# Row-wise self-attention on one core: all y adds on GpSimd, one PSUM bank per group, one output pair and the copy of g moved

## The reference

```python
xn = (x - moving_mean) * jax.lax.rsqrt(moving_var + BN_EPS) * gamma + beta
q = xn @ Wq + bq
k = xn @ Wk + bk
v = xn @ Wv + bv
scores = jnp.einsum('bhid,bhjd->bhij', q, k) * d ** (-0.5)
attn = jax.nn.softmax(scores, axis=-1)
out = jnp.einsum('bhij,bhjd->bhid', attn, v)
out = out @ Wo + bo
return xn + out
```

## Time and profile before

| | |
|---|---|
| median of 3 runs | 4906.45 us (4906.04 to 4907.05) |
| profiled execution | 4908.15 us, its span 4906.1 us |
| busy: PE, DVE, ACT, POOL | 4865.9, 4404.1, 4353.9, 4509.1 us |
| granted TensorE clock, mean | 0.999 of full speed |
| busy share of the 16 DMA engines, q1 | 82.1% |

### The profile page before, as it was taken

How to read it: one execution, slowest core, us unless ns; L and a number is a source line. 1 busy time by engine, 2 the same in 40 slices (tenths; PEclk the granted TensorE clock), 3 DMA queues, 4 the chain that set the end, 5 groups by cost and what they waited for, 6 DMA issues and landing times.

```text
span 4906.1 us, 171155 instructions
## 1 busy us (share of the span) xinstructions
PE 4865.9 (99%) x51224; PEld 4047.9 (83%) x51224; DVE 4404.1 (90%) x6946; ACT 4353.9 (89%) x18948; POOL 4509.1 (92%) x2824
## 2 busy tenths in 40 slices
PE   7999999999999999999999999999999999999999
PEld 5888888888888888888888888888888888888887
DVE  6999999999999999999999999999999999999998
ACT  6888888888898888888888888888888988888887
POOL 6999999999999999999999999999999999999997
PEclk9999999999999999999999999999999999999999
DMA  6888888888888888888888888888888888888886
GB/s 129 167 166 166 165 166 166 166 167 166 167 166 166 166 166 167 166 166 166 166 166 166 166 166 166 165 166 167 167 166 166 166 166 166 166 167 167 166 166 131
DMA packets 4294233, 806.24 MB, mean 164 GB/s; under 512 B 4294208, under 2 KB 4294208, under 8 KB 4294208
## 3 DMA queue, kind: packets, MB, share of 16 engines
q1 hardware_dynamic: 4294208, 805.93, 82.1%
HBM read 537.10 MB, written 268.44 MB: 164 GB/s over the span
## 4 chain that ended last, share of the span: by engine, by line
PE 99%; DVE 0%; ACT 0%; SPq 0%; issue 0%; DMA 0%; DVEq 0%
PE score_ps L590 21%; PE probsT_ps L625 21%; PE g_ps L635 19%; PE uo_ps L649 19%; PE u_ps L609 11%; PE uo_ps L609 9%; ACT probs L318 0%; DVE row_stat L468 0%; DMA bias_col<-in_L_conv_bv 0%; DVE uT L488 0%; ACT g L345 0%; PE u_ps L571 0%; SPq L191 0%; SPq L189 0%; SPq L193 0%
## 5 line engine op out<-in xcount | busy, mean ns | idle before, releaser
L318 ACT ACTIVATE probs<-score_ps,neg_top 128x128 f32<-128x128 f32 x8192 | 2896.8, 377 | 479.2 <-DVE neg_top L478 479.2
L265 POOL TENSOR_TENSOR x_weighted<-x_in,row_weights 128x1024 f32<-128x1024 f32 x1024 | 2401.7, 2370 | 32.1 <-DMA x_in<-in_x 32.1
L318 ACT ACTIVATION_READ_ACCUMULATOR probs<-score_ps,neg_top 128x1 f32 x8192 | 1784.0, 218 | 0.0
L468 DVE TENSOR_REDUCE row_stat<-score_ps 128x8 f32<-128x1024 f32 x1024 | 1250.5, 1221 | 188.1 <-PE score_ps L590 179.0
L287 POOL TENSOR_TENSOR y<-attn,x_scaled_rows 128x512 f32<-128x512 f32 x768 | 980.8, 1277 | 359.8 <-DVE attn L434 359.7
L649 PEld LDWEIGHTS uo_ps<-w_o,uT 128*128 128x128 f32 x8192 | 1055.0, 191 | 268.1 <-issue 265.5
L625 PE MATMUL probsT_ps<-ident,probs 128*128 128x128 f32 x8192 | 1272.3, 278 | 2.0 <-ACT probsT L333 1.4
L625 PEld LDWEIGHTS probsT_ps<-ident,probs 128*128 128x128 f32 x8192 | 925.8, 141 | 384.0 <-issue 360.3
L276 POOL TENSOR_TENSOR x_scaled_rows<-x_weighted,out_bias 128x512 f32<-128x512 f32 x1024 | 1200.7, 1200 | 0.0
L649 PE MATMUL uo_ps<-w_o,uT 128*128 128x128 f32 x8192 | 1164.8, 275 | 3.6 <-DVE uT L488 2.3
L635 PE MATMUL g_ps<-xT,w_g 128*128 128x512 f32 x2048 | 1090.4, 614 | 9.1 <-ACT g L345 5.7
(11 more groups left out here) (70 smaller groups left out, 2397.1 us busy)
## 6 DMA issues: line engine op xcount, KB each, us to landing
x_quads<-in_x SPq DMA_DIRECT2D x4096, 64.0 KB, 2.2
x_in<-in_x SPq DMA_DIRECT2D x1024, 256.0 KB, 3.2
out<-y SPq DMA_DIRECT2D x1024, 256.0 KB, 2.4
norm_row<-in_L_conv_gamma SPq DMA_DIRECT2D x1, 32.0 KB, 4.2
norm_row<-in_L_conv_beta SPq DMA_DIRECT2D x1, 32.0 KB, 4.0
norm_row<-in_L_conv_moving_mean SPq DMA_DIRECT2D x1, 32.0 KB, 4.7
norm_row<-in_L_conv_moving_var SPq DMA_DIRECT2D x1, 32.0 KB, 4.6
norm_row<-in_L_conv_bo SPq DMA_DIRECT2D x1, 32.0 KB, 4.5
```

What stands on the lines that cost most here:

```text
L265: nc.gpsimd.tensor_tensor(x_weighted[:, n % 4, :, 0:2 * C].rearrange("p s (h c) -> p s h c", h=2), x_in[:, n % 8, :, None, :].broadcast_to ...
L318: last = nc.scalar.activation(probs[:, n % 4, q, :], score_ps[n % 2][:, q // PAIRS, q % PAIRS * W:(q % PAIRS + 1) * W], ACT.Exp, bias=neg_ ...
L468: nc.vector.tensor_reduce(row_stat[:, s, :, NEG_MAX].rearrange("p (h k) -> p h k", h=2), score_ps[n % 2][:].rearrange("p h (k w) -> p h k ...
```

## The change

1. **y.** `vector_adds`, `scale_in_place`, `add_in_place` and their semaphores are gone. For all 1024 groups DVE scales PSUM into attn and POOL adds x_scaled_rows (`add_x`).
2. **Banks.** u_ps and uo_ps become uo_ps[0] and uo_ps[1]. u and output of group n both use uo_ps[n % 2]. `output` waits for its own u_kept alone; `probs_times_x` waits for attn_kept of group n-2 for both parities.
3. **Output pair.** On PE the last pair of the even group's output moves from ahead of the second projection to behind the next transposes.
4. **Copy of g.** On ACT the copy of g for group 2t+4 moves ahead by one exponential.
5. **DVE order.** `find_const` now runs ahead of the even group's scale.

```diff
         @block.gpsimd
             def step(r, t, peeled):
                 weigh(r, 2 * t + 2, peeled)
                 weigh(r, 2 * t + 3, peeled)
-                if vector_adds(2 * t - 5):
-                    add_bias(r, 2 * t + 2, peeled)
-                else:
-                    add_x(r, 2 * t - 5, peeled)
-                    add_bias(r, 2 * t + 2, peeled)
+                add_x(r, 2 * t - 5, peeled)
+                add_bias(r, 2 * t + 2, peeled)
                 add_bias(r, 2 * t + 3, peeled)
                 add_x(r, 2 * t - 4, peeled)
...
         @block.scalar
                 exponentials(r, 2 * t, peeled, range(0, 5))
                 keep_probsT(r, 2 * t - 2, peeled, 0)
-                exponentials(r, 2 * t, peeled, range(5, 7))
+                exponentials(r, 2 * t, peeled, range(5, 6))
                 keep_g(r, 2 * t + 4, peeled)
-                exponentials(r, 2 * t, peeled, range(7, 8))
+                exponentials(r, 2 * t, peeled, range(6, 8))
...
         @block.vector
-                nc.vector.tensor_tensor(attn[:, s], o_rows, inv_sum[:, s, :, None].broadcast_to([128, GROUP, C]),
+                nc.vector.tensor_tensor(attn[:, s], o_rows[n % 2], inv_sum[:, s, :, None].broadcast_to([128, GROUP, C]),
                                         ALU.mult).then_inc(attn_kept[s], 1)
...
             def step(r, t, peeled):
-                if vector_adds(2 * t - 5):
-                    scale_in_place(r, 2 * t - 5, peeled)
-                    invert_sums(r, 2 * t - 3, peeled)
-                    negate_const(r, 2 * t + 1, peeled)
-                    add_in_place(r, 2 * t - 5, peeled)
-                else:
-                    scale(r, 2 * t - 5, peeled)
-                    invert_sums(r, 2 * t - 3, peeled)
-                    negate_const(r, 2 * t + 1, peeled)
+                scale(r, 2 * t - 5, peeled)
+                invert_sums(r, 2 * t - 3, peeled)
+                negate_const(r, 2 * t + 1, peeled)
...
                 keep_probsT_b(r, 2 * t - 2, peeled)
+                find_const(r, 2 * t + 3, peeled)
                 scale(r, 2 * t - 4, peeled)
-                find_const(r, 2 * t + 3, peeled)
...
         @block.tensor
                 if exists(r, n - 2, peeled):
-                    if vector_adds(n - 2):
-                        pe.wait_ge(y_found[parts(n - 2)], uses(r, n - 2))
-                    elif bank is uo_ps:
-                        pe.wait_ge(attn_kept[parts(n - 2)], uses(r, n - 2))
-                    else:
-                        pe.wait_ge(u_kept[parts(n - 2)], uses(r, n - 2))
+                    pe.wait_ge(attn_kept[parts(n - 2)], uses(r, n - 2))
...
                 if 0 in pairs:
                     pe.wait_ge(u_kept[s], uses(r, n))
-                    if n % 2 == 0:
-                        pe.wait_ge(u_kept[parts(n + 1)], uses(r, n + 1))
-                    else:
-                        pe.wait_ge(attn_kept[parts(n - 1)], uses(r, n - 1))
...
                 transpose_probs(r, 2 * t - 2, peeled, 1)
-                output(r, 2 * t - 4, peeled, range(1, PAIRS))
+                output(r, 2 * t - 4, peeled, range(1, PAIRS - 1))
                 project(r, 2 * t + 5, peeled)
                 transpose_probs(r, 2 * t - 1, peeled, 0)
+                output(r, 2 * t - 4, peeled, range(PAIRS - 1, PAIRS))
                 output(r, 2 * t - 3, peeled, range(PAIRS))
                 transpose_probs(r, 2 * t - 1, peeled, 1)
```

More of the change, by code:

```diff
@@ L85, in build @@
         row_tmp = sb("row_tmp", [128, 3, C])
-        u_ps, g_ps, probsT_ps, uo_ps = (psum(n) for n in ("u_ps", "g_ps", "probsT_ps", "uo_ps"))
+        g_ps, probsT_ps = (psum(n) for n in ("g_ps", "probsT_ps"))
+        uo_ps = [psum(f"uo_ps{i}") for i in range(2)]
         score_ps = [psum(f"score_ps{i}", (128, 2, 512)) for i in range(2)]
@@ L115, in build @@
         attn_kept = sem_ring("attn_kept")
-        o_scaled = sem_ring("o_scaled")
         x_weighed = sem_ring("x_weighed")
@@ L177, in pipeline @@
                 step(N // BODY - 1, t, True)
-        def vector_adds(n):
-            return n % 4 == 3
         def exists(r, n, peeled):
@@ L402, in _ @@
             dve.wait_ge(pe_setup, 1)
-            chain(nc.vector.tensor_tensor(bias_fold[:], uo_ps[0:C, 0:3], bias_col[:], ALU.add))
+            chain(nc.vector.tensor_tensor(bias_fold[:], uo_ps[1][0:C, 0:3], bias_col[:], ALU.add))
             assert done[0] == FOLDED
@@ L415, in _ @@
                 p = slice(h * C, (h + 1) * C)
[L416 to L421, removed]
+                chain(nc.vector.tensor_copy(w_g[p, h, :], uo_ps[0][p, 0:C]))
+                chain(nc.vector.tensor_copy(w_o[p, h, :], uo_ps[0][p, C:2 * C]))
+            chain(nc.vector.tensor_copy(row_weights[:, 1, :], uo_ps[0][:, 2 * C:3 * C]))
+            chain(nc.vector.tensor_tensor(out_bias[:], uo_ps[0][:, 3 * C:4 * C], b_row[:], ALU.add))
+            chain(nc.vector.tensor_copy(g_bias[:], uo_ps[0][:, 4 * C:4 * C + 1]))
+            chain(nc.vector.tensor_copy(x_weighted[:, :, :, 2 * C], uo_ps[0][:, 4 * C + 1:4 * C + 2, None].broadcast_to([128, 4, GROUP])))
             assert done[0] == DVE_READY, done[0]
-            o_rows = uo_ps[:].rearrange("p (s c) -> p s c", s=GROUP)
+            o_rows = [b[:].rearrange("p (s c) -> p s c", s=GROUP) for b in uo_ps]
             def scale(r, n, peeled):
@@ L479, in find_shift, with keep_u @@
                                         ALU.add).then_inc(neg_top_found[s], 1)
-            def keep_u(r, n, peeled, bank):
+            def keep_u(r, n, peeled):
                 if not exists(r, n, peeled):
@@ L487, in keep_u @@
                     dve.wait_ge(o_made[parts(n - 2)], uses(r, n - 2))
-                nc.vector.tensor_copy(uT[:, n % 2], bank[:].rearrange("p (k w) -> p k w", k=PAIRS)) \
+                nc.vector.tensor_copy(uT[:, n % 2], uo_ps[n % 2][:].rearrange("p (k w) -> p k w", k=PAIRS)) \
                     .then_inc(u_kept[s], 1)
@@ L540, in step @@
                 find_max(r, 2 * t + 1, peeled)
-                keep_u(r, 2 * t - 4, peeled, u_ps)
-                keep_u(r, 2 * t - 3, peeled, uo_ps)
+                keep_u(r, 2 * t - 4, peeled)
+                keep_u(r, 2 * t - 3, peeled)
                 find_shift(r, 2 * t + 1, peeled)
@@ L554, in _ @@
             for i in range(3):
-                last = nc.tensor.matmul(uo_ps[0:C, i:i + 1], w_raw[:, i, :], ab_col[:, 1:2], start=True, stop=True)
+                last = nc.tensor.matmul(uo_ps[1][0:C, i:i + 1], w_raw[:, i, :], ab_col[:, 1:2], start=True, stop=True)
             last.then_inc(pe_setup, 1)
@@ L570, in _ @@
                                  (4 * C + 1, bias_wide[:, 0, :], bias_fold[:, 1:2])):
-                last = nc.tensor.matmul(u_ps[:, o:o + rhs.shape[1]], lhsT, rhs, start=True, stop=True)
+                last = nc.tensor.matmul(uo_ps[0][:, o:o + rhs.shape[1]], lhsT, rhs, start=True, stop=True)
             last.then_inc(pe_setup, 1)
@@ L576, in _ @@
             w_o_all = w_o[:].rearrange("p h c -> p (h c)")
-            o_pairs = uo_ps[:].rearrange("p (h k c) -> p h k c", h=2, k=PAIRS)
+            o_pairs = [b[:].rearrange("p (h k c) -> p h k c", h=2, k=PAIRS) for b in uo_ps]
             def scores(r, n, peeled):
@@ L592, in scores, with probs_times_x @@
                 last.then_inc(scores_made[s], 1)
-            def probs_times_x(r, n, peeled, bank):
+            def probs_times_x(r, n, peeled):
                 if not exists(r, n, peeled):
@@ L600, in probs_times_x @@
                 if exists(r, n - 2, peeled):
-                    if vector_adds(n - 2):
-                        pe.wait_ge(y_found[parts(n - 2)], uses(r, n - 2))
-                    elif bank is uo_ps:
-                        pe.wait_ge(attn_kept[parts(n - 2)], uses(r, n - 2))
-                    else:
-                        pe.wait_ge(u_kept[parts(n - 2)], uses(r, n - 2))
+                    pe.wait_ge(attn_kept[parts(n - 2)], uses(r, n - 2))
                 for k in range(PAIRS):
                     for h in range(2):
-                        last = nc.tensor.matmul(bank[h * C:(h + 1) * C, k * W:(k + 1) * W], x_in[:, n % 8, PAIRS * h + k, :],
+                        last = nc.tensor.matmul(uo_ps[n % 2][h * C:(h + 1) * C, k * W:(k + 1) * W], x_in[:, n % 8, PAIRS * h + k, :],
                                                 probsT[:, n % 2, PAIRS * h + k, :], start=True, stop=True)
@@ L643, in output @@
                     pe.wait_ge(u_kept[s], uses(r, n))
-                    if n % 2 == 0:
-                        pe.wait_ge(u_kept[parts(n + 1)], uses(r, n + 1))
-                    else:
-                        pe.wait_ge(attn_kept[parts(n - 1)], uses(r, n - 1))
                 for k in pairs:
-                    last = nc.tensor.matmul(o_pairs[:, :, k, :], uT[:, n % 2, k, :], w_o_all, start=True, stop=True)
+                    last = nc.tensor.matmul(o_pairs[n % 2][:, :, k, :], uT[:, n % 2, k, :], w_o_all, start=True, stop=True)
                 if PAIRS - 1 in pairs:
```

(4 more changed lines are left out.)

## The result

The changed kernel takes **4875.48 us** (median of 4, 4874.62 to 4876.16) against 4906.75 (4906.04 to 4907.82) in the same comparison: ratio 0.9936, interval 0.9919 to 0.9953. That is 31 us less; the forecast was 44 less, 4862, with a range of 4846 to 4892. The profiled execution took 4876.16 us.

A forecast was written before the change was run, and what follows sets the result against it. No engine was full; a ring over PE, DVE and ACT took 9.471 us per step. Longest of ring 9.36, POOL 9.385 and PE 9.32 decides: 512 x (9.471 - 9.385) = 44 us less, 4862 us, range 4846 to 4892.

The forecast's parts named there:

- The ring: Chain of waits over PE, DVE and ACT from scores to next scores: 9.471 us per step, to become 9.36.
- the distances 0.86, 0.34 and 0.04: PE's second projection to next group 0.86; ACT's last exponential to second copy of probsT 0.34; PE's projection end to g 0.04.
- The 0.60 for the copy: On ACT, the time taken for the late copy of probsT, before PE's second transposes start 0.14 later.
- the 0.11 forecast: On ACT the late copy of probsT starts 0.11 earlier, shortening the step from 9.471 to 9.36 us.
- POOL's pace: GpSimd steps with both adds take 9.385 us, the longest, so they decide: 4856 to 4872, chance 0.60.
- the signs: Trace marks to check, among them POOL steps of 9.38 to 9.39 and DVE's find_const waiting for weigh late on.
- the rival of the torn cover: ACT waits 0.05 to 0.08 more for g_ps; ring 9.41 to 9.44, 4875 to 4890 us, chance 0.12.
- y on POOL at nothing: POOL's new add is hidden by today's idle time; DVE losing its in-place y is worth nothing directly.
- The hidden edits: find_const ahead of the scale costs nothing per step; separate banks worth 0, perhaps 1 us in the last step.
- that thin cover: On ACT the earlier copy of g waits 0.02 for PE; a result 0.1 later would lose ACT that 0.1.
- The rival "does nothing": Scores, maximum and exponentials alone make 9.47 per step, so the pace stays: 4906 us, chance 0.08.
- "Slower by POOL": POOL is full and stands idle before its second add because attn comes 1.3 later: 4945 us, chance 0.08.

The follow-up runs named there:

- The small op: Changed kernel plus one 128x16 add on GpSimd in every step, writing a tile that nobody reads: 4956.99 us.
- the relief: Changed kernel, but for each eighth group VectorE scales in PSUM and adds y instead of GpSimd: 4874.79 us.
- the first experiment: Kernel before the change with only the copy of g moved one exponential earlier: 4879.60 us.
- the control: Kernel before the change with only the copy of g moved, plus the same extra 128x16 GpSimd add in every step: 4881.22 us.
- the try with the later copies: Changed kernel with ACT's first copy of probsT and copy of g one exponential later, and the second output pair ahead of the second transposes: 4902.12 us.
- the kernel before: The kernel without the change: 4906.75 us in the comparison with the changed kernel.
- the second experiment: Changed kernel with the copy of g put back behind two exponentials: 4977.81 us.

## Why the prediction was right, and where it was off

**The ring** of scores, neg_top, exponentials, copy of g, late projection, late transposes, late copy of probsT and scores was right: moving the copy of g alone gives 29.7 of 31.3 us, and the distances 0.86, 0.34 and 0.04 came out as forecast. One sentence of the prediction contradicts it: VectorE, which makes the maximum and neg_top, is on the ring. Only its in-place y wasn't.

**Its length was mis-sized**, 9.36 forecast, and 9.40 measured within one step (2467.64 to 2477.04), 9.414 on average. The late copy of probsT starts 8.07 after the scores (8.06 by the sum), but PE's transposes follow its start by 0.77, not 0.74. The 0.60 for the copy came from a row in which it had waited; directly behind an exponential it lasts 0.62. The 0.01 to the average is the longer fourth step. So the ring lost 0.057 per step (9.471 to 9.414), half of the 0.11 forecast; by its own figure the time would have come out 0.054 x 512 = 28 us too low. Against the 9.385 that decided the sum it is 0.029 x 512 = 15 us, and 13 were measured. That the miss isn't larger is luck: POOL's figure, wrong as the bound, lay nearer to the true step than the ring's. Of the 31.3 us the steps account for 512 x (9.471 - 9.414) = 29; the other 2 lie outside the steps of mid-kernel and weren't traced.

**POOL's pace** of 9.385 was a right figure, but it wasn't the bound: the step of the sum that failed is "decides: 9.385", where the ring's 9.414 decided. The small op puts POOL 0.02 below the pace, and the relief shows that it isn't the bound. Two of the signs failed with it: POOL's steps aren't 9.38 to 9.39, and DVE has no wait for weigh late in the kernel. The chance for this case, 4856 to 4872, 0.60, was too high for two bounds 0.025 apart, taken from rows read to 0.01; the measured 4875.48 lies outside it. What came is nearest to the rival of the torn cover (9.41 to 9.44, 4875 to 4890), though not by its mechanism: ACT doesn't wait longer for g_ps than the 0.04.

**y on POOL at nothing** was right (-0.8). **The hidden edits.** find_const was right at 0. The pair had no price of its own; it is worth 0 to 3 us. That the pair costs if g is late wasn't in the prediction; it named that thin cover only for ACT. The banks weren't tried alone. With one bank for both outputs the odd group's, right behind the moved pair, would have to wait for the even group's attn; what that costs wasn't measured.

**The rival "does nothing"** (the late copy of probsT wasn't what held PE) falls with the first experiment. **"Slower by POOL"** didn't come; with 0.18 more work on POOL it does, through find_const and not through its idle time before y.

## What to carry to other kernels

Where no engine is full and each waits a little, follow the starts around one period: an instruction that comes later than its engine's usual distance, and just behind the end of another engine's, is a link of the ring, even if the list of waits shows nothing. Work in the queue ahead of a wait is free as long as it ends before the wait does; the same work behind it is part of the ring. With g late, one output pair behind the projection instead of ahead of it came with 68.5 us more; with g in time its place was worth at most 3. When two bounds come out closer than the rows are exact, add a little to one and take a little from it: together these tell which one holds and how much is to spare.

## What the runs showed that I had not expected

POOL's row durations aren't the time that an instruction adds to its queue. With POOL as the bound the small op is listed with 1.20 us while the next starts 0.18 later, and two weighs with 5.67 though the instruction behind them starts after 4.64; in the control the same rows read 0.23 and 4.69. Yet the listed end counts for those that wait: find_const starts at 2476.08, 0.11 behind the weighs' listed end (2470.30 + 5.67 = 2475.97), though POOL began its next y at 2474.94. So a POOL that never waits hands on its results about 1 us later than one that does, at the same distance from start to start. Why is open. ScalarE's rows do something like it: exponentials start 0.34 apart throughout, and are listed with 0.36 right behind a wait and with 0.43 at the end of a stretch without one:

```profile
2472.71 0.36 ACT L311 ACTIVATE probs<-score_ps,neg_top 128x128 f32<-128x128 f32 x1
...
2477.22 0.43 ACT L311 ACTIVATE probs<-score_ps,neg_top 128x128 f32<-128x128 f32 x1
```

Sums of these durations overstate what both engines need; for the pace the distance from start to start held, for those that wait the listed end.

PE loses more by a wait than its length: in the try with the later copies it waited 0.10 for g and then took 0.94 for a projection that takes 0.86 otherwise. In the kernel before it is 0.93 behind a wait of 0.03, in the second experiment 0.93 behind one of 0.26. The loss is 0.07 to 0.08 each time, whatever the length of the wait; what it consists of wasn't traced.
